# Cross-attention on one core: wholly masked queries by a 78th key scored from the mask's rows, and a first q load issued from two queues

## What is computed

```python
q = _split_heads(query, W_Q); k = _split_heads(key, W_K); v = _split_heads(value, W_V)
scores = jnp.einsum('bhqd,bhkd->bhqk', q, k) / np.sqrt(D_K)
scores = jnp.where(mask[:, None, :, :] == 1, jnp.float32(-1000000000.0), scores)
p = jax.nn.softmax(scores, axis=-1)
ctx = jnp.einsum('bhqk,bhkd->bhqd', p, v)
out = jnp.einsum('bsd,ed->bse', concat, W_O) + residual
mu = jnp.mean(out, axis=-1, keepdims=True)
var = jnp.mean((out - mu) ** 2, axis=-1, keepdims=True)
return (out - mu) * jax.lax.rsqrt(var + LN_EPS) * gamma + beta
```

## Time and profile before

| | |
|---|---|
| runs | 181.10, 182.79, 183.29 us (median 182.79) |
| profiled execution | 183.17 us, span 181.4 us |
| TensorE's mean granted clock | 0.988 |
| PE busy | 160.0 us, 88% of the span |
| DVE busy | 136.5 us, 75% |
| ACT busy | 100.5 us, 55% |
| POOL busy | 95.8 us, 53% |
| DMA | 30.17 MB, mean 166 GB/s |

### The profile page before, as it was taken

The page is one execution under the profiler, slowest core; times in us unless marked ns, Lnnn a source line. Parts: engine busy times, 40 slices in busy tenths (PEclk is TensorE's granted clock), DMA queues, the critical chain, the costliest instruction groups (busy, mean ns, idle before and its releaser), DMA issues.

```text
span 181.4 us, 3507 instructions
## 1 busy us (share of the span) xinstructions
PE 160.0 (88%) x1224; PEld 87.0 (48%) x1224; DVE 136.5 (75%) x303; ACT 100.5 (55%) x134; POOL 95.8 (53%) x119
## 2 busy tenths in 40 slices
PE   7798878889699999999999999999899799799830
PEld 7555544343344554455545554554356364164520
DVE  0858757684978499778977897789989985758991
ACT  3224155563475655558755875586667458796400
POOL 7000750330743451249576957664954675895692
PEclk9999999999999999999999999999999999999995
DMA  5959958768767977872797575656541024011205
GB/s 174 350 144 169 260 86 222 208 143 246 195 173 239 268 223 222 266 195 48 212 264 188 179 209 133 190 159 197 148 173 64 4 107 129 0 59 61 116 0 231
DMA packets 21829, 30.17 MB, mean 166 GB/s; under 512 B 3436, under 2 KB 17356, under 8 KB 21812
## 3 DMA queue, kind: packets, MB, share of 16 engines
q1 hardware_dynamic: 20692, 28.19, 54.8%
q10 hardware_dynamic: 1120, 1.76, 2.9%
HBM read 11.28 MB, written 4.19 MB: 85 GB/s over the span
## 4 chain that ended last, share of the span: by engine, by line
PE 57%; DVE 11%; DMA 9%; issue 7%; POOL 7%; ACT 6%; SPq 1%; POOLq 0%; ACTq 0%; DVEq 0%
PE pv_ps L885 13%; PE work_ps L824 11%; PE work_ps L895 11%; PE scores_ps L876 9%; PE max_ps L845 8%; DMA x_t<-in_x_cols 4%; DVE neg_max L631 4%; DMA R<-neg_max_t 3%; DVE ctx_q L639 2%; DMA R<-q 2%; PE scores_ps L824 2%; POOL y L372 2%; ACT probs L526 2%; POOL y L378 1%; DVE first_max L631 1%
## 5 line engine op out<-in xcount | busy, mean ns | idle before, releaser
L526 ACT ACTIVATE probs<-scores_ps 77x1024 f32<-77x1024 f32 x60 | 60.5, 1017 | 43.7 <-PE scores_ps L876 38.4
L631 DVE TENSOR_REDUCE neg_max<-max_ps 128x6 f16<-128x462 f32 (+1 forms) x84 | 45.4, 565 | 11.9 <-PE max_ps L845 11.8
L845 PEld LDWEIGHTS max_ps<-kb,R 125*128 125x128 f16 x512 | 26.2, 98 | 34.4 <-DVE neg_max L631 17.8
L344 POOL TENSOR_TENSOR q<-q 128x512 f16<-128x512 f32 x14 | 16.2, 1155 | 49.5 <-ACT q L487 49.5
L876 PE MATMUL scores_ps<-R,kb 126*77 126x512 f16 x120 | 36.1, 384 | 1.0 <-DMA R<-neg_max_t 1.0
L845 PE MATMUL max_ps<-kb,R 125*128 125x77 f16 x512 | 31.9, 199 | 4.3 <-DVE neg_max L631 3.3
L885 PE MATMUL pv_ps<-probs,v_all 77*32 77x512 f32 x248 | 33.0, 604 | 2.6 <-ACT probs L526 1.5
L351 POOL TENSOR_TENSOR ctx_n<-ctx_q,rden 128x256 f32<-128x256 f32 x31 | 19.4, 627 | 23.9 <-DVE rden L641 23.6
L639 DVE STREAM_TRANSPOSE ctx_q<-pv_ps 128x512 f32<-128x512 f32 x31 | 22.0, 709 | 9.8 <-PE pv_ps L885 9.4
L895 PE MATMUL work_ps<-wo_t,ctx_e 128*128 128x256 f32 x112 | 27.0, 384 | 0.1
L824 PE MATMUL work_ps<-x_t,wq_t 128*128 128x512 f32 x48 | 23.6, 614 | 0.4
(11 more groups left out here) (88 smaller groups left out, 149.0 us busy)
## 6 DMA issues: line engine op xcount, KB each, us to landing
...
out<-y ACTq DMA_DIRECT2D x2, 256.0 KB, 2.0
...
```

Of the source, the lines that this page charges most:

```text
L344: nc.gpsimd.tensor_tensor(q16[:, e, 1, :], q32[:, e, :], q16[:, e, 0, :], ALU.subtract).then_inc(q_low, 1)
L526: nc.scalar.activation(probs[:, s, :, :], scores_ps[scores_buffer(PAIRS * n + s)[0]][0:KEYS, :, :], ACT.Exp).then_inc(exp_done, 1)
L631: nc.vector.tensor_reduce(to[:, t, lo:hi], max_ps[u % 2][:, 0:(hi - lo) * KEYS].rearrange("p (h k) -> p h k", k=KEYS), AX.X, ALU.max, nega ...
L845: last = nc.tensor.matmul(max_ps[u % 2][:, (h - lo) * KEYS:(h - lo + 1) * KEYS], R[m % R_RING][0:MAX_ROW, h, t * P:(t + 1) * P], kb[0:MAX_ ...
```

## The change

- **A 78th key.** `COLS` is 78. The mask value is 32768 instead of 61440. `kb`'s column 77 holds 256/32768 against each mask row, zeros against q and against the maximum, and 64 - 77*256 against a new row of ones in `R` (`one_row`, row 126). Its score is thus 64 when all 77 keys are masked, and at most -192 otherwise, so that its weight is then 0. Its value row is the mean of the value rows, from a 78th context column that DVE makes: `sum_ctx` (a reduction over 2x4x77 numbers a partition) and `mean_ctx` (128x4, twice).
- **Gone:** all 8 `count` matmuls, all 8 `nf` activations, the 16 `q_scale` products, `q32`, and POOL's 14 `q_lo` subtractions.
- **q's split:** `q_hi` on ACT reads the bank of `project_q`; `q_lo` on DVE subtracts it from the same bank. PE's next use of `work_ps` waits for `q_low` where it waited for `q_scaled`. ACT's `q_hi` now stands ahead of the exponential of its step, and DVE's `q_lo` behind the first reductions of its step.
- **Mask to fp16:** blocks 5 to 7 move from POOL to DVE, at step 6 of n = 1 to 3 (`eq_late`).
- **Queues:** in the head ACT's queue issues the high parts of k and q of half 1 (four DMAs) that SP's queue did. SP issues four row loads more there and one later, and loads W_O (256 KB) in n = 0, where ACT's queue did at 11.2 us.
- **POOL's order** changes: `norm` moves ahead of `plus_beta` and of `moments`.
- Shapes grow by one: 78 columns or partitions in `scores`, exp and `values`, 127 rows in `scores`; `max_unit` keeps 125 rows and 77 columns.

```diff
+ONE_ROW = MAX_ROW + 1
+ROWS = ONE_ROW + 1
+BIG = 32768.0
+
+
+PER_KEY = 256.0
+WHOLE = 64.0
...
-            sp.wait_ge(consts, 1)
-            sp.dma_start(kb_flat[MAX_ROW:ROWS, :].rearrange("p (n k) -> p n k", k=KEYS),
-                         ones16[0:1, 0:KEYS].unsqueeze(1).to_broadcast([1, HEADS * BATCH, KEYS])).then_inc(tail_ones, 16)
             load_k(0, 0)
-            load_k(0, 1)
+            load_k_low(0, 1)
             load_q(0, 0)
-            load_q(0, 1)
+            load_q_low(0, 1)
+            sp.wait_ge(rows_ready, 5)
+            load_last_row(0)
+            load_last_row(1)
+            load_one_row(0, s_last_rows)
+            load_one_row(1, s_last_rows)
...
+                if n == 0:
+                    sp.dma_start(wo_t[:, :, :], w_o).then_inc(s_wo, 16)
...
-            def q_lo(m, e):
-                pool.wait_ge(q_high, HALVES * m + e + 1)
-                nc.gpsimd.tensor_tensor(q16[:, e, 1, :], q32[:, e, :], q16[:, e, 0, :], ALU.subtract).then_inc(q_low, 1)
...
+            pool.memset(last_rows[:, 0, :, 0:KEYS], 1.0).then_inc(rows_ready, 1)
+            pool.memset(last_rows[:, 0, :, KEYS:COLS], 0.0).then_inc(rows_ready, 1)
+            pool.memset(last_rows[:, 1, :, 0:KEYS], 0.0).then_inc(rows_ready, 1)
+            pool.memset(last_rows[:, 1, :, KEYS:COLS], WHOLE - KEYS * PER_KEY).then_inc(rows_ready, 1)
...
+            norm(N - 2, 0)
             plus_beta(N - 5, 0)
-            norm(N - 2, 0)
             plus_beta(N - 5, 1)
+            norm(N - 2, 1)
             moments(N - 4)
-            norm(N - 2, 1)
             times_gamma(N - 4, 0)
...
-            def nf(m):
-                act.wait_ge(count_done, m + 1)
-                if m >= 2:
-                    act.wait_ge(q_scaled, HALVES * (m - 1))
-                nc.scalar.activation(not_full[m % 2][:, :], work_ps[:, :], ACT.Sign, bias=all_keys[:, :], scale=-1.0
-                                     ).then_inc(nf_ready, 1)
-
-            def q_hi(m, e):
-                act.wait_ge(q_scaled, HALVES * m + e + 1)
+            def q_hi(m, e, bank):
+                act.wait_ge(q_done, HALVES * m + e + 1)
                 if m > 0:
                     act.wait_ge(s_R[(m - 1) % R_RING][e], loaded_R(m - 1))
-                nc.scalar.activation(q16[:, e, 0, :], q32[:, e, :], ACT.Copy).then_inc(q_high, 1)
+                nc.scalar.activation(q16[:, e, 0, :], bank, ACT.Copy).then_inc(q_high, 1)
...
+            act.wait_ge(k_high, HALVES)
+            for part in (0, 1):
+                act.dma_start(q_rows(kb_rows, part, PER_HALF, HEADS)[:, :, 0:PAIR_KEYS], k16[:, 0, 1, 0:PAIR_KEYS]).then_inc(s_kb[0][1], 16)
+            q_hi(0, 0, q_ps[0][0])
+            q_hi(0, 1, q_ps[0][1])
+            act.wait_ge(q_high, HALVES)
+            for part in (0, 2):
+                act.dma_start(q_rows(R[0], part, PER_HALF, HEADS), q16[:, 1, 0, :]).then_inc(s_R[0][1], 16)
             v_copy(0)
...
+                    if n == 0 and s in (2, 4, 6):
+                        q_hi(2 + s // 6, s // 2 - 1 if s < 6 else 0, work_ps[:, :])
+                    if n == 1 and s == 0:
+                        q_hi(3, 1, work_ps[:, :])
+                    if n >= 1 and n + 3 < N and s in (2, 4):
+                        q_hi(n + 3, s // 2 - 1, work_ps[:, :])
                     exp(n, s)
                     if n == 0:
                         if s == 1:
                             turn_first_max(2)
...
-            def q_lo(m, e):
+            def q_lo(m, e, bank):
                 dve.wait_ge(q_high, HALVES * m + e + 1)
-                nc.vector.tensor_tensor(q16[:, e, 1, :], q32[:, e, :], q16[:, e, 0, :], ALU.subtract).then_inc(q_low, 1)
-
-            def q_scale(m, e, bank):
-                dve.wait_ge(q_done, HALVES * m + e + 1)
-                dve.wait_ge(nf_ready, m + 1)
-                if m > 0:
-                    dve.wait_ge(q_low, HALVES * (m - 1) + e + 1)
-                nc.vector.tensor_tensor(q32[:, e, :], bank, not_full[m % 2][:, :], ALU.mult).then_inc(q_scaled, 1)
+                nc.vector.tensor_tensor(q16[:, e, 1, :], bank, q16[:, e, 0, :], ALU.subtract).then_inc(q_low, 1)
+
+            def sum_ctx():
+                dve.wait_ge(s_ctx, 16)
+                nc.vector.tensor_reduce(ctx_sum[:, :, :], ctx_tb[:, :, :, 0:KEYS], AX.X, ALU.add).then_inc(ctx_summed, 1)
+
+            def mean_ctx(p):
+                dve.wait_ge(ctx_summed, 1)
+                dve.wait_ge(k_done, HALVES * (p + 1))
+                nc.vector.tensor_scalar(ctx_tb[:, :, 2 * p:2 * p + 2, KEYS], ctx_sum[:, :, 2 * p:2 * p + 2], 1.0 / KEYS, None, ALU.mult
+                                        ).then_inc(ctx_mean, 1)
+
+            def eq_late(m):
+                dve.wait_ge(s_mask[m % 2], 16 * (m // 2 + 1))
+                for e in range(HALVES):
+                    dve.wait_ge(s_R[(m - 2) % R_RING][e], loaded_R(m - 2))
+                nc.vector.tensor_scalar(eq16[m % 2][:, :], mask_i[m % 2][:, :], 1.0, BIG, ALU.is_equal, ALU.mult
+                                        ).then_inc(eq_ready, 1)
...
-                    if n == 0 and s in (2, 4):
-                        q_scale(2, s // 2 - 1, work_ps[:, :])
-                    if n == 0 and s == 6:
-                        q_scale(3, 0, work_ps[:, :])
...
+                    if n == 0 and s in (2, 4, 6):
+                        q_lo(2 + s // 6, s // 2 - 1 if s < 6 else 0, work_ps[:, :])
+                    if n >= 1 and n + 3 < N and s in (2, 4):
+                        q_lo(n + 3, s // 2 - 1, work_ps[:, :])
...
+                    if s == 6 and 1 <= n and n + 4 < N:
+                        eq_late(n + 4)
...
-            def count(m):
-                pe.wait_ge(eq_ready, m + 1)
-                nc.tensor.matmul(work_ps[:, :], ones16[:, :], eq16[m % 2][:, :], start=True, stop=True).then_inc(count_done, 1)
...
+                if b == 0:
+                    pe.wait_ge(ctx_mean, i + 1)
...
                     if 1 <= n and n + 3 < N:
-                        if s == 0:
+                        if s == 1:
                             if n >= 2:
                                 pe.wait_ge(out_ready, 2 * (n - 1))
                             else:
-                                pe.wait_ge(q_scaled, 4 * HALVES)
-                            count(n + 3)
-                        if s == 1:
-                            pe.wait_ge(nf_ready, n + 4)
+                                pe.wait_ge(q_low, 4 * HALVES)
                             project_q(n + 3, 0, work_ps[:, :])
                         if s == 3:
-                            pe.wait_ge(q_scaled, HALVES * (n + 3) + 1)
+                            pe.wait_ge(q_low, HALVES * (n + 3) + 1)
```

More of the change, by code:

```diff
@@ L52 @@
 NM_FIRST = 5
-PAIR_KEYS = 2 * KEYS
+PAIR_KEYS = 2 * COLS
 LOADS_R = 4
@@ L269, in load_k, with load_k_low @@
                     sp.dma_start(q_rows(kb_rows, part, lo, hi)[:, :, pair], k16[:, 0, e, pair]).then_inc(s_kb[p][e], 16)
+                load_k_low(p, e)
+            def load_k_low(p, e):
+                lo, hi = e * PER_HALF, (e + 1) * PER_HALF
+                pair = slice(p * PAIR_KEYS, (p + 1) * PAIR_KEYS)
                 sp.wait_ge(k_low, HALVES * p + e + 1)
@@ L412, in _ @@
                     times_gamma(n - 3, 1)
+                norm(n, 0)
                 if n >= 3:
                     plus_beta(n - 3, 0)
-                if n + 3 < N:
-                    q_lo(n + 3, 0)
-                norm(n, 0)
+                norm(n, 1)
                 if n >= 3:
                     plus_beta(n - 3, 1)
-                if n + 3 < N:
-                    q_lo(n + 3, 1)
                 if n >= 2:
                     moments(n - 2)
-                norm(n, 1)
-                if n + 4 < N:
-                    eq(n + 4)
                 norm(n, 2)
@@ L705, in _ @@
             spread_mask(0, 1)
-            q_scale(0, 0, q_ps[0][0])
+            sum_ctx()
+            mean_ctx(0)
+            q_lo(0, 0, q_ps[0][0])
             eq(1)
-            q_lo(0, 0)
-            q_scale(0, 1, q_ps[0][1])
-            q_lo(0, 1)
+            q_lo(0, 1, q_ps[0][1])
             spread_mask(1, 0)
-            q_scale(1, 0, q_ps[1][0])
             spread_mask(1, 1)
             k_lo_second()
-            for u in range(TILES):
-                reduce_max(0, u)
+            mean_ctx(1)
+            reduce_max(0, 0)
+            reduce_max(0, 1)
+            q_lo(1, 0, q_ps[1][0])
+            reduce_max(0, 2)
+            reduce_max(0, 3)
             reduce_max(0, TILES)
             reduce_max(0, TILES + 1)
-            q_scale(1, 1, q_ps[1][1])
             reduce_max(0, TILES + 2)
+            q_lo(1, 1, q_ps[1][1])
             reduce_max(0, TILES + 3)
@@ L732, in _ @@
                     if n == 1 and s == 0:
-                        q_scale(3, 1, work_ps[:, :])
+                        q_lo(3, 1, work_ps[:, :])
                     if s == 0 and n >= 2:
                         residual(n - 2, 1)
```

(13 more changed lines are left out.)

136 lines of the change are left out of this document (58 added, 78 removed).

## The result

The changed kernel ran in 184.45, 184.74, 187.16 and 188.87 us, median 185.95; the kernel before, with one more run of it, in 183.04. The ratio is 1.0145, 95% interval 1.0079 to 1.0211; medians count every execution, ratios leave out those more than 1.5% above the fastest of their kernel (here 188.87 and, before, 186.94). So the change makes the kernel slower by 1.5 to 2%, some 2.7 to 4 us, where 183.4 us (+0.6) was forecast; 185.95 lies above the range. The profiled execution took 187.16 us, span 185.4, against 183.17 and 181.4.

The account below looks back on a forecast made before the run. PE was taken to bound n = 1 to 4, order of waits the rest. 183.17 - 1.65 - 0.1 + 1.1 + 1.25 = 183.8 us, or 183.4 from the median; eight in ten 180.6 to 185.2.

Parts of the forecast that it names:

- Steady blocks: In n = 1 to 4, PE without count and the flag wait gains 0.41 us a block, -1.65 us.
- The head: Before n = 0, an earlier start is nearly offset by two added steps: between -0.8 and +0.1, taken as -0.1 us.
- n = 0: At step 2, q_lo delays DVE's transpose and the row of maxima; block 1 starts at 51.2, not 50.11: +1.1 us.
- n = 6: moments behind norm(6,1) make ACT's apply 1.3 us late, and PE waits for the exponentials behind it: +1.25 us.
- The port pair: Rival: DVE's eq_late and POOL contend for ports, or the row lands late: 184.6 to 185.5 us, chance 0.17.
- the rule in the prediction: Trainium skill: such a DVE operation and GpSimd share a port pair; the first holds it, the other fully blocks.
- `q_hi` never waited for the rows of the block before: Rival: q_hi waits for the previous block's rows in four blocks; 1 us late gives 187.4 us, chance 0.09.
- The losses don't come: Rival: row landing hides n = 0's loss, apply's wait is absorbed: 181.0 us, or 182.2 with one loss; chance 0.28.

Follow-up runs that it names:

- e4: The changed kernel with ACT's high part of q(2,0) moved ahead of turn_first_max(2) and its DMA issue in n = 0: 187.07 us, ratio 1.0180.
- e1: The changed kernel with block 4's moments put back ahead of norm(6,1) on POOL in n = 6: 183.17 us, ratio 0.9967.
- e9: The changed kernel run again without an edit, against the kernel before: 187.52 us, ratio 1.0217.
- e3: The changed kernel with 16 and 20 products of zeros in PE's idle stretches before scores(7,1) and values(6,3): 185.25 us, ratio 1.0109.
- e12: The kernel before with moments moved behind norm(6,1) in n = 6 and products of zeros in PE's idle stretches: 184.74 us, ratio 1.0057.
- e2: The kernel before with only moments moved behind norm(6,1) on POOL in n = 6: 186.74 us, ratio 1.0185.

## Why the prediction was wrong, step by step

- **Steady blocks: right.** The 1.91 us by which block 1 started late (52.02 against 50.11) were gone by n = 4: -0.51 and -0.53 us a block instead of -0.41. Copies 2 to 4 lie 17.79 and 17.76 us apart, 18.30 and 18.29 before. The window of the changed kernel beside the earlier trace rows:

```profile
88.19:105.95 17.76, 17.67 (x141) 9.43 (x140) 15.48 (x36) 11.52 (x15) 9.15 (x13) 1.00 0.76 215
```

DVE at 15.48 is below PE, as said (15.7). The gain was taken 0.3 us too small in all.

- **The head: nearly right.** PE's first maxima started at 16.30, 0.9 us sooner than before, and most of the gain was lost behind `q_hi(1,1)`: the next transposes came 0.34 us sooner (25.69 against 26.03). But one wait wasn't in the sum. ACT's issue of the first row took 1.48 us and the row landed at 26.4, PE waited 0.45 us for it: `scores(0,0)` at 26.52, +0.17 instead of -0.1.

- **n = 0: right in its mechanism, short by 0.6** (block 1 started 0.8 us later than forecast, 0.2 of it from the head). Timeline of ACT, DVE and PE in the changed kernel, beside the earlier trace rows:

```profile
32.01 0.62 ACTq L519 DMA_DIRECT2D R<-first_max_t  x1
32.73 0.60 ACT L496 ACTIVATE q<-work_ps 128x512 f16<-128x512 f32 x1 [0.75 <-ACT first_max_t L517]
33.36 0.69 DVE L617 TENSOR_TENSOR q<-work_ps,q 128x512 f16<-128x512 f32 x1 [1.42 <-ACT q L496]
33.97 0.70 DVE L653 STREAM_TRANSPOSE ctx_q<-pv_ps 128x512 f32<-128x512 f32 x1
...
35.60 0.37 PE L859 MATMUL max_ps<-kb,R 125*128 125x77 f16 x6 [1.54 <-DVE neg_max L645]
```

PE's wait of 0.74 became 1.54, the transpose starts 0.95 late, the row was issued at 45.20 (forecast 45.2). Its landing was taken as 5.9 us, the slowest of before, and took 6.8: block 1 at 52.02, not 51.2. e4 confirmed the first half (-0.79 us when `q_hi` goes first). The second half is the spread of one DMA: e1's landed in 6.1 us and block 1 started 2.70 us behind the maxima that waited 1.57 us, 3.39 in the change; e9's landed in 4.3.

- **n = 6: the step that failed.** The prediction let `apply` start at 152.35, let PE's wait at 154.94 grow with it, and added 1.25 us. That was right where it stood: `apply` started at 152.41, `values(6,3)` at 156.34, 1.40 late. What was wrong is that the sum stopped there, with a wait priced at its own length and everything behind it at its old durations; TensorE's clock stands in no term, no rival and not in the range. PE had already been idle 1.00 us at that place; the change made it 0.97 and 1.26 with a single pair of `scores` between. The clock fell, and 6.8 us of n = 7 ran at 1.2 GHz. The term was +3.96, of which the prediction had 1.25. The runs show each half alone: 1.43 us for the wait (e3 against e1, e12 against the kernel before), 2.52 and 2.34 for the clock (the change against e3, e2 against e12).

Sum by the profiled executions, against +0.6 forecast: head +0.17, n = 0 +1.74, steady blocks -1.94, n = 6 and 7 +3.96, in all +3.93 of 3.99 measured. Of the 3.3 us that the forecast lacks 2.7 are the term of n = 6, 0.6 that of n = 0 and 0.3 the head's, less 0.3 of the steady blocks.

- **The rivals.** The port pair did not show. In n = 3 DVE and POOL, side by side:

```profile
104.05 0.36 DVE L633 TENSOR_SCALAR eq<-mask_i 77x512 f16<-77x512 int32 x1
```

```profile
104.21 0.68 POOL L374 TENSOR_TENSOR ctx_n<-ctx_q,rden 128x256 f32<-128x256 f32 x1 [1.02 <-DVE rden L655]
```

`eq_late` took 0.36 us, less than the 0.42 allowed, and `norm` 0.68 for 0.62: POOL paid 0.06. The two overlapped for 0.20 us, from 104.21 to 104.41, so POOL wasn't blocked for all of it, as it would be by the rule in the prediction. `q_hi` never waited for the rows of the block before: of the 14.3 us that ACT idled ahead of its twelve in the loop, 12.9 were for PE and the rest ACT's own order. "The losses don't come" fell, since both came. No rival had the clock in it. The time of the port rival (184.6 to 185.5) was near the measured one, 0.5 us short of it, for a wrong reason.
